# Expert choice and slots inside attention's first pairs, two scalings on VectorE

## What is computed

```python
xn = (x - mu) / jnp.sqrt(var + 1e-05) * gamma + beta      # second layer, attention
q = xn @ Wq; k, v = jnp.split(xn @ Wkv, 2, axis=-1)       # 16 heads of 64
q = apply_rope(pos, q); k = apply_rope(pos, k); q = q * SCALE
sim = jnp.where(causal_mask, neg, jnp.einsum('bhid,bhjd->bhij', q, k))
out = jnp.einsum('bhij,bhjd->bhid', softmax(sim), v) @ Wo
...
scores_BSN = jnp.einsum('bsd,nd->bsn', x, Wr) + br        # second layer, experts
w_BSN = softmax(scores_BSN)
_, idx_BSK = jax.lax.top_k(scores_BSN + biases_N, 2)      # 2 of 8 experts
val_BSK = take_along_axis(w_BSN, idx_BSK); val_BSK = val_BSK / sum(val_BSK)
```

## Time and profile before

| | us |
|---|---|
| median of 3 runs (2678.33 to 2678.72) | 2678.37 |
| the profiled execution's own time | 2666.09 |
| its span | 2664.3 |
| PE busy in the span | 2461.2 (92%) |
| DVE busy | 1291.0 (48%) |
| ACT busy | 1128.3 (42%) |
| POOL busy | 552.0 (21%) |

### The profile page before, as it was taken

One profiled execution on the slowest core, in us unless ns is written; L12 is line 12 of the kernel. 1 busy time (PEld: TensorE's weight loads), 2 busy tenths in 40 slices (PEclk: granted clock), 3 DMA queues, 4 the chain that ended last, 5 costly groups with the idle time before them and its releaser, 6 DMA issues. The chain is left out here.

```text
span 2664.3 us, 45788 instructions
## 1 busy us (share of the span) xinstructions
PE 2461.2 (92%) x14584; PEld 1697.2 (64%) x14585; DVE 1291.0 (48%) x3175; ACT 1128.3 (42%) x2597; POOL 552.0 (21%) x505
## 2 busy tenths in 40 slices
PE   5999996999994599999999999999999998999993
PEld 4454544555553366666666666666666667999993
DVE  5445452222226465665565565566565653333334
ACT  3112111111113366666666666666666663222222
POOL 3000002444426233332111111111111110111113
PEclk9999998999996799999999999999999999999997
DMA  5011012876435432232111121112222215767696
GB/s 204 16 40 39 25 38 96 260 219 184 120 71 166 138 109 79 90 97 74 31 41 45 39 63 42 36 39 55 56 56 55 55 52 185 237 237 238 239 342 224
DMA packets 145741, 295.47 MB, mean 111 GB/s; under 512 B 16800, under 2 KB 102704, under 8 KB 135312
## 3 DMA queue, kind: packets, MB, share of 16 engines
q1 hardware_dynamic: 124736, 251.79, 29.6%
q0 software_dynamic: 20944, 42.94, 6.2%
HBM read 194.00 MB, written 67.12 MB: 98 GB/s over the span
## 5 line engine op out<-in xcount | busy, mean ns | idle before, releaser
L1510 DVE CUSTOM_DVE_ANT_0 at_p<-at_ps,atk_mask 128x640 f32<-128x640 f32 (+7 forms) x512 | 375.8, 753 | 258.7 <-PE at_ps L1374 146.7
L1421 ACT ACTIVATE at_p<-at_p,at_nmax 128x640 f32<-128x640 f32 (+7 forms) x512 | 391.6, 768 | 59.2 <-DVE at_nmax L1510 59.2
L1428 ACT ACTIVATE at_pT<-at_ps 128x512 f32<-128x512 f32 (+1 forms) x640 | 325.6, 554 | 201.7 <-PE at_ps L1374 201.4
L1453 POOL TENSOR_TENSOR at_qkT<-at_raw,at_swapped 128x1024 f32<-128x1024 f32 x64 | 150.7, 2355 | 1024.2 <-DVE at_swapped L1525 1024.2
L1374 PEld LDWEIGHTS at_ps<-atk_ident,at_p 128*128 128x128 f32 x2304 | 255.6, 141 | 137.8 <-issue 127.6
L1540 DVE SCALAR_TENSOR_TENSOR late_y<-at_ps,at_inv,late_y 128x256 f32<-128x256 f32 x512 | 215.1, 477 | 222.4 <-PE at_ps L1395 204.0
L1374 PE MATMUL at_ps<-atk_ident,at_p 128*128 128x128 f32 x2304 | 314.7, 278 | 2.0 <-ACT at_p L1421 2.0
L1364 PE MATMUL at_ps<-at_qkT 64*128 64x512 f32 (+3 forms) x1536 | 292.9, 500 | 7.9 <-POOL at_qkT L1453 3.8
L1385 PE MATMUL at_ps<-at_pT,at_v 128*64 128x256 f32 (+1 forms) x2560 | 277.7, 363 | 0.0
L1346 PE MATMUL at_ps<-atk_h,atk_w 128*128 128x512 f32 x512 | 242.0, 596 | 19.1 <-SPq L1220 19.1
L1385 PEld LDWEIGHTS at_ps<-at_pT,at_v 128*64 128x64 f32 x2560 | 172.4, 137 | 99.7 <-issue 21.8
(11 more groups left out here) (233 smaller groups left out, 3234.0 us busy)
## 6 DMA issues: line engine op xcount, KB each, us to landing
moe_w<-in_w_w SPq DMA_DIRECT2D x53, 1028.0 KB, 4.9
at_swapped<-at_raw SPq DMA_DIRECT2D x256, 128.0 KB, 2.4
late_w<-in_w_w SPq DMA_DIRECT2D x18, 1028.0 KB, 4.8
atk_w<-in_w_qkv SPq DMA_DIRECT2D x32, 384.0 KB, 3.1
slot_in<-ex_zero SPq DMA_DIRECT2D x9, 1032.0 KB, 9.2
ex_wg<-in_w_eg SPq DMA_DIRECT2D x16, 512.0 KB, 3.4
ex_wu<-in_w_eu SPq DMA_DIRECT2D x16, 512.0 KB, 4.7
ex_wd<-in_w_ed SPq DMA_DIRECT2D x16, 512.0 KB, 6.7
```

The costliest lines, as they stand in the source:

```text
L1421: act.activation(buf, buf, ACT.Exp, bias=nmax[:, unit:unit + 1], scale=-1.0, accum_out=rsum[:, unit:unit + 1]).then_inc(exp_done, 1)
L1428: act.activation(dst, ring[RING_BANK[part][ev]][:, 0:(i1 - i0) * P].rearrange("p (k c) -> p k c", c=P), ACT.Copy).then_inc(t_read, 1)
L1453: pool.tensor_tensor(out=qkT[x][:, :].rearrange("p (m t) -> p m t", m=2)[:, :, half * CH:(half + 1) * CH], in0=raw[half][:, :].rearrange(" ...
L1510: dve.tensor_tensor_reduce(out=p[unit % LAG][:, 0:(n[0] + 1) * P], in0=scores(*n), in1=mask[:, T - (n[0] + 1) * P:T], scale=-1.0, scalar=3 ...
```

## The change

- The exponential, the two matmuls and VectorE's whole chain of lines 453 to 508, but for the addition of `br` to the logits (now into `d.sc`), leave `renormalize`. They stand in `attention` as a function `route(stage)` with six stages. Stages 0 to 3 stand as words R0 to R3 in a new table for the first part, `DVE_FIRST`; stage 4 stands ahead of pair 0's M4.0, stage 5 ahead of its M5.0. The matmuls stand in `PE_FIRST` as R0 ahead of S0, and A7 of pair 0 is now ahead of S0 too. The exponential is R0 in `ACT_FIRST`. Their scratch lies in `moe_w2`, behind the rows.
- Stage 5 compares with seven independent `tensor_scalar` and one reduction, where seven dependent instructions stood.
- `rescaled` of groups 6 and 7 goes from ScalarE to VectorE.
- GpSimd loads both row buffers at the start and sends rows in pairs 1 to 8. In pair 8 the second four sends stand behind `end(0)`.
- The loops: pairs 0 and 1 are written out ahead of a loop over pairs 2 to 7, and the loop over sequences then starts at 1.
- SP waits for `known` before it reads the first expert.

```diff
+                def rescaled(g):
+                    dve.wait_ge(r2_made, g // 2 + 1 + ONE)
+                    dve.wait_ge(scaled_ps, 2 * (g - 1) + ONE)
+                    for i in range(GT):
+                        at = g * GT + i
+                        ins = dve.tensor_scalar(scaled[g % 2][:, i * C:(i + 1) * C], stage[g % 4][:, i * C:(i + 1) * C],
+                                                r2[:, at:at + 1], None, ALU.mult)
+                    ins.then_inc(scaled_late, 1)
...
+                for g in range(G - 2, G):
+                    rescaled(g)
                 dve.wait_ge(log_ps, G + ONE)
-                do(dve.memset(ones[:, :], 1.0))
-                do(dve.tensor_tensor(out=te(sc), in0=LOG[:, 0:W].rearrange("p (t e) -> p t e", e=E1), in1=over_t(br), op=ALU.add))
...
-                do(dve.tensor_copy(d.tile_expert[:, :], eid[(E1 - 1) % 2][:, :]))
+                dve.tensor_tensor(out=te(d.sc), in0=LOG[:, 0:W].rearrange("p (t e) -> p t e", e=E1), in1=over_t(br), op=ALU.add)
...
-                pe.wait_ge(masks, 1 + ONE)
-
-                pe.matmul(ps[0][:, 0:W], before[:, :], both[:, :], start=True, stop=True)
-                pe.matmul(ps[1][:, 0:W], ones[:, :], both[:, :], start=True, stop=True).then_inc(counted, 1)
...
                 for g in range(G - BEHIND, G):
-                    if g > G - BEHIND:
-                        rescaled(g)
...
+PE_FIRST = "A0+ A1+ A2+ A3+ A4+ A5+ A6+ A7+ R0+ S0+ S1+"
+ACT_FIRST = "A0+ A1+ R0+ A4+ A5+ E0.0+ E0.1+ E1.0+ E1.1+"
+DVE_FIRST = "R0+ A2+ A3+ R1+ P0+ P1+ A6+ A7+ R2+ M0.0+ M0.1+ P2+ M1.0+ M1.1+ P3+ R3+"
+ROUTE_AHEAD_OF = {("M", (4, 0), 0): 4, ("M", (5, 0), 0): 5}
+FIRST = {PE_ORDER: PE_FIRST, ACT_ORDER: ACT_FIRST, DVE_ORDER: DVE_FIRST}
...
-                with eng.Fori(0, nb - 1) as b:
+                for u in range(2):
+                    act_on("both", u, u, u, 0)
+                with eng.Fori(1, PAIRS // 2) as i:
+                    for u in range(2):
+                        act_on("both", i * 2 + u, i * 2 + u, u, 0)
+                with eng.Fori(1, nb - 1) as b:
...
+                        elif kind == "R":
+                            pe.wait_ge(masks, 1 + ONE)
+                            pe.matmul(ps[6][:, 0:W], before[:, :], both[:, :], start=True, stop=True)
+                            pe.matmul(ps[6][:, W:2 * W], ones[:, :], both[:, :], start=True, stop=True).then_inc(counted, 1)
...
+                            if isinstance(of, int) and of == 0 and n == 0:
+                                pe.wait_ge(slots_read, 1 + ONE)
...
                 load_rows(0)
+                load_rows(1)
                 pool.wait_ge(numbered, 16 + ONE)
                 for of in range(nb * PAIRS):
                     rotate(of, 0)
+                    j = of - 1
+                    if 0 <= j < TOP * B:
+                        if j == 0:
+                            pool.wait_ge(routed, 1 + ONE)
+                        else:
+                            pool.wait_ge(sent, 16 * TB * j)
+                            if j + 1 < TOP * B:
+                                load_rows(j + 1)
+                        at = j // B * NT + j % B * TB
+                        pool.tensor_copy(row_parts(j)[:, :, C], d.tok_w[:, at:at + TB])
+                        pool.tensor_copy(row_parts(j)[:, :, C + 1], number[:, at:at + TB]).then_inc(marked, 1)
+                        pool.wait_ge(marked, j + 1 + ONE)
+                        pool.wait_ge(rows_in[j % 2], 16 * (j // 2 + 1))
+                        send(j, range(0, TB // 2))
...
+                def choose(k):
+
+                    do(dve.tensor_reduce(out=sums, in_=te(bi), axis=AX, op=ALU.max))
+                    do(dve.tensor_tensor(out=te(tmp), in0=te(bi), in1=bcast(sums, E1), op=ALU.is_equal))
+                    do(dve.tensor_tensor(out=te(tmp), in0=te(tmp), in1=over_t(rank), op=ALU.mult))
+                    do(dve.tensor_reduce(out=sums, in_=te(tmp), axis=AX, op=ALU.max))
+                    do(dve.tensor_tensor(out=te(m[k]), in0=over_t(rank), in1=bcast(sums, E1), op=ALU.is_equal))
...
+                def route(stage):
+                    if stage == 0:
+                        do(dve.memset(ones, 1.0))
+                        do(dve.tensor_reduce(out=top, in_=te(sc), axis=AX, op=ALU.max))
+                        dve.tensor_tensor(out=te(w_r), in0=te(sc), in1=bcast(top, E1), op=ALU.subtract).then_inc(less_max, 1)
+                        do(dve.tensor_tensor(out=te(bi), in0=te(sc), in1=over_t(bias), op=ALU.add))
+                        choose(0)
+                        do(dve.scalar_tensor_tensor(out=bi, in0=m[0], scalar=-3.0e38, in1=bi, op0=ALU.mult, op1=ALU.add))
+                    elif stage == 1:
+                        choose(1)
+                        dve.tensor_tensor(out=both, in0=m[0], in1=m[1], op=ALU.add).then_inc(masks, 1)
+                        do(dve.memset(line, 1.0))
+                    elif stage == 2:
+                        dve.wait_ge(expd, 1 + ONE)
+                        do(dve.tensor_reduce(out=sums, in_=te(w_r), axis=AX, op=ALU.add))
...
+                    elif stage == 3:
+                        dve.wait_ge(counted, 1 + ONE)
+                        do(dve.tensor_copy(et(tot), ps[6][:, W:2 * W].rearrange("p (t e) -> p e t", e=E1)))
+                        do(dve.tensor_tensor_scan(out=run_, data0=line, data1=tot, initial=0.0, op0=ALU.mult, op1=ALU.add))
+                        do(dve.tensor_reduce(out=cnt, in_=et(tot), axis=AX, op=ALU.add))
...
+                        do(dve.tensor_tensor(out=run_, in0=run_, in1=tot, op=ALU.subtract))
+                    elif stage == 4:
+                        dve.tensor_tensor(out=te(slot), in0=ps[6][:, 0:W].rearrange("p (t e) -> p t e", e=E1),
+                                          in1=run_.rearrange("p (e t) -> p t e", t=NT), op=ALU.add).then_inc(slots_read, 1)
+                        dve.wait_ge(slots_read, 1 + ONE)
+                        do(dve.tensor_tensor(out=te(slot), in0=te(slot), in1=over_t(offs), op=ALU.add))
...
+                        ins.then_inc(routed, 1)
+                    else:
+                        for e in range(E1 - 1):
+                            last = dve.tensor_scalar(past[:, e * SLOT_TILES:(e + 1) * SLOT_TILES], tile_no[:, :], end[:, e:e + 1], None, ALU.is_ge)
+                        do(last)
+                        do(dve.tensor_reduce(out=eid, in_=past[:, 0:(E1 - 1) * SLOT_TILES].rearrange("p (e t) -> p t e", t=SLOT_TILES), axis=AX, op=ALU.add))
+                        dve.tensor_copy(d.tile_expert[:, :], eid).then_inc(known, 1)
```

More of the change, by code:

```diff
@@ L408, in _ @@
                 st = Steps(dve, steps)
-                def do(ins):
-                    st.done(ins)
-                    st.wait()
                 def add_moe(g):
@@ L476, in _ @@
-                do(dve.tensor_tensor(out=sums[:, :], in0=wk[0][:, :], in1=wk[1][:, :], op=ALU.add))
-                do(dve.reciprocal(sums[:, :], sums[:, :]))
-                for k in range(TOP):
-                    st.done(dve.tensor_tensor(out=d.tok_w[:, k * NT:(k + 1) * NT], in0=wk[k][:, :], in1=sums[:, :], op=ALU.mult))
-                dve.wait_ge(counted, 1 + ONE)
-                do(dve.tensor_copy(et(tot), ps[1][:, 0:W].rearrange("p (t e) -> p e t", e=E1)))
-                do(dve.memset(line[:, :], 1.0))
@@ L1124, in part_of @@
 def part_of(order, part):
-    return [ev for ev in events(order) if part == "both" or ev[2] == (part == "first")]
+    if part == "first":
+        return events(FIRST[order])
+    return [ev for ev in events(order) if part == "both" or not ev[2]]
 def ring_uses(part):
@@ L1171, in scores, with scratch, te, et @@
             return s.all_banks[:, at:at + (t + 1) * P]
+        W = NT * E1
+        at = 2 * TB * ROW
+        def scratch(cols):
+            nonlocal at
+            at += cols
+            return d.moe_w2[:, at - cols:at]
+        before, bias, rank, tile_no = d.at_route
+        sc, bi, w_r, tmp, slot, both, tot, run_, line = d.sc, *(scratch(W) for i in range(8))
+        m = [scratch(W) for k in range(TOP)]
+        ones, top, sums, slot_f = scratch(P), scratch(NT), scratch(NT), scratch(TOP * NT)
+        wk = [scratch(NT) for k in range(TOP)]
+        cnt, til, end, offs, past, eid = (scratch(n) for n in (E1, E1, E1, E1, E1 * SLOT_TILES, SLOT_TILES))
+        cnt_i = s.sb("cnt_i", E1, I32)
+        assert at <= E1 * KH * C
+        steps, less_max, expd, masks, counted, slots_read, routed, known = (s.sem(x) for x in (
+            "steps", "less_max", "expd", "masks", "counted", "slots_read", "routed", "known"))
+        def te(ap):
+            return ap[:, :].rearrange("p (t e) -> p t e", e=E1)
+        def et(ap):
+            return ap[:, :].rearrange("p (e t) -> p e t", t=NT)
+        def over_t(ap):
+            return ap[:, :].unsqueeze(1).to_broadcast([P, NT, E1])
         if scatter:
@@ L1297, in _ @@
                 moe_weights(PAIRS - 1)
+                sp.wait_ge(known, 1 + ONE)
```

(1 more changed line is left out.)

118 lines of the change are left out of this document (44 added, 74 removed).

## The result

The changed kernel takes 2659.46 us (median of 4 runs, 2658.5 to 2661.71) against 2678.35 (4 runs): ratio 0.9933, 95% interval 0.9921 to 0.9946, so 18.9 us faster. The forecast was 2665.7 and its range ended at 2661.8: the sign was right, the gain too small. Its interval is 14.5 to 21.2 us.

The account below looks back on a forecast made before the run. TensorE, busy 92%, was taken as the bound, with a 19.1 us wait for attention's start. A start 15.9 us earlier less 3.2 paid back gives 12.7: 2678.37 - 12.7 = 2665.7 us, range 2661.8 to 2670.5.

Parts of the forecast that it names:

- Part 1: End of `renormalize`: without the expert-choice chain and with rescaling on VectorE, attention starts 15.9 us earlier; bounds 13.0 and 16.5.
- Part 2: Start of attention: the six stages, 20.1 us of VectorE, fit into its idle times; net cost about 0.
- Part 3: Delay of M2.0 in attention: VectorE held by GpSimd's rotations 2.9 us, late exchange 0.4; 3.3 in sum, 3.2 paid.
- (a): Rival: VectorE isn't held by GpSimd in attention's start; 15.6 us faster, 2662.8; chance 0.22.
- The late exchange: Attention's start: the exchange of halves beside the second row load delays P0 by 0.4 us; bounds 0 and 2.2.
- Any delay of M2.0 is paid one for one: Pair 0 of attention: a delay of M2.0 from another cause reaches S6 in full, less 0.1 us.
- (b): Rival: a second drop of TensorE's clock or a late exchange adds; 2669.7 to 2671.7, middle 2670; chance 0.15.
- The sends one pair later: GpSimd's row sends in attention: moving them costs nothing, as GpSimd is idle in most of a pair.
- (d): Rival: engines stand while code of the two written-out pairs is fetched; slower than before, needing 18.1 us; chance 0.04.

Follow-up runs that it names:

- psum_ops: Changed kernel with one PSUM operand in stage 2's first multiplication and in stage 3's scan, the counts' copy moved to stage 2: 2659.55 us (0.9931).
- all_three: Changed kernel with the two operands in PSUM, sends in twos, and the second row load behind the first rotation: 2650.60 us (0.9901).
- after_third: The changed kernel measured again, unedited, on the third chip: 2653.91 us (0.9941).
- act_scales: Changed kernel with the rescaling of groups 6 and 7 back on ScalarE: 2665.58 us (0.9963).
- before_shift1: Kernel before with its sends one pair later, in fours, and GpSimd's new list but for the wait for `routed`: 2669.11 us (0.9999).
- before_again: The kernel before measured again, unedited, for a second trace: 2676.15 us (1.0001).
- after_again: The changed kernel measured again, unedited, for a second trace: 2661.96 us (0.9950).
- all_three_b: Repeat on the third chip of the changed kernel with PSUM operands, sends in twos and later second load: 2649.62 us (0.9925).
- after_late9: Changed kernel with GpSimd's row sends moved to pairs 9 to 16: 2663.16 us (0.9950).
- sends_2x2: Changed kernel with GpSimd's 64 sends in twos, two behind each rotation, over pairs 1 to 16: 2653.91 us (0.9911).

## Why the prediction fell short, by its own steps

**Part 1, the block's start, 15.9 us: right.** 16.35 by the traces, inside its bounds (13.0 to 16.5). Its half for the rescaling was 2.9 and is 3.6; VectorE waited for TensorE's transposes of group 5 as said ([5.01 <-PE] at L434), and ScalarE evicted group 7's halves without a gap behind group 6.

**Part 2, the stages: right but for stage 5.** The working had M5 1.2 to 1.4 us later and 1.0 in hand at S6, so next to nothing to pay. Stage 5 takes 2.6 us, not 2.1 (seven comparisons 1.25, the reduction 1.06, the cast 0.20), and S6 waits 0.91 us for VectorE behind it. psum_ops and all_three have this wait too, and it is paid (41.4 us for all_three's pair 0).

**Part 3, the held VectorE, 2.9 us: right**, 0.94 + 1.91 = 2.85 by the two durations (1.36 against 0.42, 2.60 against 0.69, the lengths of their kind in the profiles of the two kernels). psum_ops shows the cause for the multiplication; for the scan it is read from its end, 0.54 us behind the rotation's, and from its 2.60 us in every trace of the changed kernel. (a) falls. **The late exchange, 0.4: mis-sized.** P0 waited 1.26 us behind stage 1, and 1.39 in psum_ops; all_three, with the load behind the first rotation, has 0.16.

**"Any delay of M2.0 is paid one for one", less 0.1: a term was missing**, the one of (b). TensorE's clock does drop behind the stand ahead of T2. Stretches of after_third and of psum_ops from T2 on (us, busy times of PE, PEld, DVE, ACT, POOL, granted clock, DMA share, GB/s):

```profile
923.00:925.50 2.50, 2.42 (x12) 2.42 (x13) 2.29 (x7) 1.11 (x3) 0.00 (x0) 0.56 0.35 80
```

```profile
922.00:924.50 2.50, 2.48 (x18) 2.02 (x20) 2.29 (x7) 1.43 (x3) 0.00 (x0) 1.00 0.36 84
```

0.56 is close to the lower of the two levels (1.2 of 2.4 GHz), after an idle 2.89 us; in psum_ops TensorE stood 1.49 us and kept the full clock. It costs 1.7 us over T2, A6 and S4 (1.92 us for eight matmuls that took 1.06 in before), of which 1.3 arrive at S6. act_scales parts this from the held VectorE: both instructions are held there as well and M2.0 comes 28.4 us after the memset, yet TensorE, slower in the projections ahead (A4 2.95 us), stands for less and keeps its clock.

```profile
925.90 0.65 PE L1337 MATMUL at_ps<-atk_ident,at_p 128*128 128x128 f32 x4 [2.15 <-ACT at_raw L1403]
926.39 1.06 PE L1315 MATMUL at_ps<-atk_w,atk_h 128*128 128x128 f32 x8
```

The granted clock is 1.00 from 926.00 to 928.50. S6 follows M2.0 after 16.4 us there and in psum_ops, and after 17.7 to 18.0 in the traces of the changed kernel.

Together, from the memset to pair 1's first scores the changed kernel needs 61.65 us, and the forecast was 55.2 + 3.2 = 58.4. Against before_shift1 the loss is 4.4 us: M2.0 is 3.1 us later (28.6 us after the memset, not 25.5), and S6 another 1.2 behind it. So the terms that the sum had come to about 12.0 us against its 12.7: they do not explain a gain of 18.9.

**The step that failed is the starting point: the first trace of before was taken for its typical execution, and all that stood outside parts 1 to 3, the sends' move among it, was put at nothing.** The prediction carried the 12.3 us between that profile and the median over "for reasons outside the change". They were partly inside. No other trace of before has its 55.2 us: there are 57.2 to 57.7 in four, and 60.7 in before_again. Its 2666.09 us do not belong to one of the timed executions either (2676.02 to 2678.72), as they do in every later run. No execution of before on chips A and B took less than 2674.66 us, while on chip C the lowest took 2666.55. So the first profile looks like one from a chip without the hold, set against a median from a chip with it; the record cannot settle this. Two things were missing in it.

First, the projections right behind the block's start. In before_shift1:

```profile
909.01 6.69 PE L1346 MATMUL at_ps<-atk_h,atk_w 128*128 128x512 f32 x8 [19.12 <-SPq L1220]
```

6.25 to 6.72 us in five traces of before, 5.06 in the first, and 5.25 to 5.90 in ten of the changed kernel and its variants, after a wait of 7.8 to 8.3 us instead of 19.1. The length of the wait is not all of it: in act_scales they take 6.42 us after 7.8 us, where TensorE had stood twice just ahead, for the scaled rows (2.92 and 2.46 us; once, 2.50, in the changed kernel). The granted clock in these stretches, of before_shift1 and after_third:

```profile
909.01:915.50 6.49, 6.49 (x8) 2.65 (x9) 1.55 (x1) 0.60 (x1) 1.81 (x2) 0.53 0.71 230
```

```profile
891.80:897.40 5.60, 5.60 (x9) 2.37 (x10) 5.33 (x11) 0.60 (x1) 1.79 (x2) 0.62 0.69 219
```

They take about 1 us less in the changed kernel, a gain that is inside the 4.4 us above. The sum had no such gain, since the first trace of before, with its 5.06, showed none to be had.

Second, on some chips, the hold of the sends. "The sends one pair later" stood among the edits at nothing. With before_again and after_again, both from chip A, the parts add up to the whole: memset 908.60 - 892.08 = 16.5 earlier; to pair 1's first scores 60.7 against 61.7, 1.0 lost, since before pays 3.4 us there for eight sends in a row and the next four (60.7 against 57.3); then 1.3 lost up to the last pair, as the changed kernel has more of its sends still to come; and 2.25 less in the rest. The sum is 16.5, the difference of the spans, 2675.2 - 2658.7. By these two traces the sends' move is worth 3.4 - 1.3, about 2 us, where the hold exists, and 0 where it doesn't. The medians do not bear the 2 us out: the gain is 14.0 us with the sends at one place in both kernels and 13.9 with the move, and both are 2.2 to 2.6 us below the 16.2 and 16.5 us between the profiled executions. Of the first measurement's 18.9 us, then, 2.4 remain even over the 16.5. Whether they are chance (16.5 is inside the interval) stays open. A gain of 13.9 to 15.5, as later measured, would have been inside the forecast's range.

On chip C, without the hold, the two places that the change touches give the 12.0 us of above, 16.35 - (61.65 - 57.3), against medians 15.2 and 15.5 lower, with 12 to 19.5 inside the interval. The rest isn't found in one place: from the last pair's first scores to the end the traces of before take 487.7 to 491.8 us, those of the changed kernel 486.2 to 488.1, with no new wait in `moe`. Whether that is a gain of the change or chance stays open. So does what the hold is: ScalarE, VectorE and TensorE all start instructions late whose releaser is done, behind the fourth send in a row on two chips and not on the third.

Rival (d) is out: every wait of TensorE in pairs 0 and 1 has another engine as its releaser, and pair 1, written out, takes 40.4 us in after_third like those in the loop.

## What to carry to other kernels

Before a sum is made against a profile, compare its own time with the median of the runs: 0.46% apart, 12.3 us, was as much as the whole forecast gain, and it hid two costs that the change touches. A second trace of the kernel before shows at least the first of them. Work that moves into holes of VectorE beside a long GpSimd instruction was held here with two SBUF inputs (1.36 us for 0.42, 2.60 for 0.69) and, as a `tensor_scalar`, with one (1.36 for 0.17), so putting one operand in PSUM may only shift the hold to the next instruction; look through the whole stretch of the rotation. Indirect DMAs in long rows were best spread, two at a time, which was worth 8 us on chip B and cost nothing on chip C.

## What the runs showed of the hardware

- A `TENSOR_SCALAR` on 8 columns with one SBUF input waits for a GpSimd instruction that runs: 1.36 us for 0.17. So in psum_ops; 1.38 and 1.37 in all_three and all_three_b. A reduction (0.42 us) and a multiplication with one of its inputs in PSUM (0.42 us), both inside a rotation, do not wait.
- Behind four indirect DMAs of 128 rows issued in a row, instructions of other engines start 0.3 (VectorE) to 0.7 us (ScalarE) late in after_late9, and pairs are longer on chips A and B, not on C. Behind eight, in before_again, VectorE starts 2.2 us late. With two in a row no pair is longer (sends_2x2 and all_three on chip B). The same program differs by 7 to 8 us between such chips.
- Ahead of T2, stands of 1.49 us (psum_ops) and 2.15 us (act_scales) cost TensorE no clock and one of 2.89 us did (1.00 granted over the next 2.5 us in psum_ops, 0.56 in after_third; what TensorE did ahead of the stand differed too). Behind the block's start TensorE had 0.53 granted over 6.5 us in before_shift1 and 0.62 over 5.6 us in after_third.
